# Edge gathers asked for by pairs of tiles, at most 24 tiles ahead, in a two-layer graph network kernel

## Chip, cores and metric

The kernel runs on one core of a Trainium2 chip (trn2). The metric is the device time of one execution in microseconds; three runs of the kernel before gave a median of 3993.59 us.

## The reference

There are 50000 nodes with 128 features and 50000 edges. A first convolution and two message-passing layers all work on the same edge list, which is sorted by destination. Each of the three sums rows over the edges of a destination node:

```python
dst = jnp.minimum((50000 * jax.random.uniform(key3, (50000,)) ** 2.0).astype(jnp.int32), 49999)
_o = jnp.argsort(dst, stable=True)
...
# convolution
h = X * norm_src
agg = jax.ops.segment_sum(h[src], dst, num_segments=N)
...
# each of the two layers
m = jnp.concatenate([h[row], h[col]], axis=-1)
m = jax.nn.relu(m @ msg_W1[l].T + msg_b1[l])
m = m @ msg_W2[l].T + msg_b2[l]
agg = jax.ops.segment_sum(m, col, num_segments=h.shape[0])
upd = jnp.concatenate([h, agg], axis=-1) @ upd_W[l].T + upd_b[l]
h = _layer_norm(h + upd, ln_g[l], ln_b[l])
```

The square in the draw of the destinations makes low node numbers much more frequent: of the blocks of 128 nodes, those at the high end have about 64 edges each and those at node 0 over a thousand.

## The kernel before

The program is a row of stages with a barrier between any two: `rank` and `place` sort the edges, `plan` makes tables, `edges` (the sum of the convolution, with the degrees), `conv`, `nodes`, then `edges0`, `nodes0`, `edges1`, `nodes1`. The three edge stages are one function, `edge_stage` (L764), called with `degrees` true for the first and false for the other two.

The edges stand in TP = 392 **edge tiles** of 128, in the order of their destinations, from the high node numbers to the low ones. The nodes stand in 392 node tiles of 128. A **step** is one edge tile with one node tile that it touches, so there are 784 steps, and four of them make one of the NB = 196 **batches** in which TensorE works. Where nodes have few edges (the start of a stage) a batch uses little more than one new edge tile; where they have many (its end) it uses nearly four.

For each edge tile GpSimd issues one indirect DMA (L851) that gathers the 128 source rows, by index, from a table in memory to a place in `ring`, which has RE = 64 places. So tile e takes the place of tile e - 64 and has to wait until that one is used up. GpSimd works through groups g of four tiles (L842 to L855). From group 16 on it first waits (L847) for the semaphore of the batch in which the last tile of group g - 16 ends; that is `s_seg` in the degrees stage and `s_pq`, which L1013 raises, in the others. The batch numbers come from the table `tile_end`, packed three to a word, of which eight words are loaded every 24 groups (L846). `tile_end` is made in `plan_stage` (L695 to L702) from `full` (L640) and a small matmul (L742), one entry per group. After the four gathers of group g it waits until group g - 2 has landed and tells TensorE so with `s_prow` (`landed`, L838 to L840). After the last group it does this for the last two.

In the degrees stage the first 48 tiles (PRE) were gathered in `plan` (L564) and GpSimd starts with tile 48.

TensorE waits in each batch for `s_prow` at the group of the newest tile it needs (L1007, L1033). In edges0 and edges1 a batch i is `segment(i - 2)` (L1021, eight matmul records) and then `combine(i)` (L1011 and L1012, sixteen records). In the degrees stage it is `sum_rows(i)` (L1036, eight records) with, in turn, a transpose of input rows (L1044) or a product with a weight (L1051) that belong to the convolution. VectorE adds the batch's four results into `acc` (L883) and makes the one-hot tiles (L868), ScalarE makes the turned one-hots and the messages.

Of the kernel before, what the change touches and what calls it, by code (L numbers as in the profile page):

```python
# [5 lines left out]
F32, F16, I32 = mybir.dt.float32, mybir.dt.float16, mybir.dt.int32  # L6
ALU, ACT, AX = mybir.AluOpType, mybir.ActivationFunctionType, mybir.AxisListType

P = 128
# [7 lines left out]
TP = 392  # L17
# [7 lines left out]
NCHUNK = TP // J  # L25
# [13 lines left out]
EW = -(-NCHUNK // 3)  # L39
EPS = 1e-5  # L40
# [475 lines left out]
def plan_stage(nc, m):  # L516

    K = TP // 4
    with ExitStack() as ctx:
# [10 lines left out]
        bound = sb("bound", [K, NCHUNK])  # L530
        cnt_w = sb("cnt_w", [K, 4, P])
        ended, ended1, at_e = sb("ended", [K, 4, S]), sb("ended1", [K, 4, S]), sb("at_e", [K, 4, S], F16)
        full = sb("full", [K, 4, NCHUNK])
# [4 lines left out]
        tf, ends = sb("tf", [1, 3, NCHUNK]), sb("ends", [1, 4, 3 * EW], I32)  # L538
# [10 lines left out]
        with nc.Block() as block:  # L549

            @block.gpsimd
            def _(pool):
# [6 lines left out]
                nc.gpsimd.iota(bound[:], pattern=[[4 * P, NCHUNK]], base=4 * P, channel_multiplier=0,  # L559
# [10 lines left out]
            def _(dve):  # L570
# [51 lines left out]
                nc.vector.memset(m.tile_end[:], 0)  # L622
# [69 lines left out]
                link(nc.vector.tensor_scalar(tf[:, 2, :], sen_row[0:1, 1:1 + TP].rearrange("o (c j) -> o c j", j=4)[:, :, 3], 1.0, None, ALU.add))  # L692
                link(nc.vector.tensor_copy(ends[:, 0, 0:NCHUNK], tf[:, 2, :]))
                dve.wait_ge(s_full, 1)
                link(nc.vector.tensor_scalar(tf[:, 0, :], ps_c[0:1, 2, 0:NCHUNK], float(TP - 1), -1.0, ALU.min, ALU.add))  # L695
                link(nc.vector.scalar_tensor_tensor(out=tf[:, 1, :], in0=bound[0:1, :], scalar=1.0 / P, in1=tf[:, 0, :],
                                                    op0=ALU.mult, op1=ALU.add))
                link(nc.vector.tensor_copy(ends[:, 1, 0:NCHUNK], tf[:, 1, :]))
                link(nc.vector.tensor_scalar(ends[:, 2, 0:NCHUNK], ends[:, 1, 0:NCHUNK], 2, None, ALU.arith_shift_right))
                link(nc.vector.tensor_scalar(ends[:, 3, 0:NCHUNK], ends[:, 2, 0:NCHUNK], 1, None, ALU.add))  # L700
                for k, to in ((0, m.chunk_end), (3, m.tile_end)):
                    pack(to[:, 0:EW], 10, [ends[:, k, :].rearrange("o (w j) -> o w j", j=3)[:, :, j] for j in range(3)], 10)  # L702

            @block.tensor
            def _(pe):
# [35 lines left out]
                for k in range(4):  # L741
                    last = nc.tensor.matmul(ps_c[:, 2, 0:NCHUNK], ones[0:K, :], full[:, k, :], start=k == 0, stop=k == 3)  # L742
# [21 lines left out]
def edge_stage(nc, m, table, table_q, agg, degrees, x=None):  # L764
# [6 lines left out]
    with ExitStack() as ctx:  # L771
# [26 lines left out]
        with nc.Block() as block:  # L798
# [35 lines left out]
            def _(pool):  # L834
# [7 lines left out]
                for g in range(first, NCHUNK):  # L842
                    if g >= RE // 4:
                        k = g - RE // 4
                        if k % 24 == 0:
                            ends = load(mybir.EngineType.Pool, m.tile_end[0:1, k // 3:k // 3 + 8])  # L846
                        pool.wait_ge(s_seg if degrees else s_pq, third(ends, k))  # L847
                        pool.sem_inc(s_go, 1)
# [705 lines left out]
```

## Time and profile before

| | us |
|---|---|
| three runs | 4000.14, 3985.41, 3993.59 (median 3993.59) |
| span of the profiled execution, first to last instruction | 3444.6 |
| median less the span | 549.0 |
| TensorE busy | 2975.2 (86%) |
| VectorE busy | 2700.0 (78%) |
| ScalarE busy | 2379.7 (69%) |
| GpSimd busy | 1846.0 (54%) |
| edges stage, by its gathers | 544.5 to 1003.4 |
| edges0 stage, by its gathers | 1577.4 to 2101.3 |
| edges1 stage, by its gathers | 2532.3 to 3056.9 |

The profile is of one execution and comes with its span; it has no device time of its own, so the three runs stand in the table. What lies outside the span is start and end of the execution. Times in the trace are counted from the span's start. Busy time leaves out waits on semaphores and register work. A GpSimd record of L851 is the making of one gather, not the landing of its data. POOL is GpSimd, PE is TensorE, DVE is VectorE, ACT is ScalarE, SP is SyncE, and a "q" behind a name is the engine's instruction queue.

### The profile page before, as it was taken

To read this page: it belongs to the slowest core of one execution; us is meant where nothing else is said; L and a number is where in the kernel's file an instruction comes from. 1 tells how busy PE (TensorE), PEld (TensorE's weight loads), DVE (VectorE), ACT (ScalarE), POOL (GpSimd) and SP (SyncE) were. 2 spreads that over 40 slices of the span, in tenths; PEclk is the share of its full clock that TensorE was granted. 3 is DMA by queue.
4 is the path that set the end of the run, shared out by engine and by line. 5 is a ranking of instruction groups with operands and counts; after the bars stand their busy time and mean duration, and the time that the engine had idled before them with its cause. 6 is when DMAs were issued, how large, how long until landed. Compare 5 with 4: busy or idle time off the path is not lost. (4 is left out here: it accounts for less than half of the span.)

```text
span 3444.6 us, 92529 instructions
## 1 busy us (share of the span) xinstructions
PE 2975.2 (86%) x25312; PEld 2674.1 (78%) x25312; DVE 2700.0 (78%) x8634; ACT 2379.7 (69%) x5642; POOL 1846.0 (54%) x1782
## 2 busy tenths in 40 slices
PE   4975656777767789997999998999979999989998
PEld 3753334555543378987999998999979999989998
DVE  9999967888856688885777776666657777769998
ACT  3779945777742368886777775666657777759999
POOL 0000036577755533335776776555547767766664
PEclk9999988999979989999999999999989999999999
DMA  0027635777649989997776654999977766548887
GB/s 21 2 69 229 223 103 162 221 219 215 195 139 340 346 280 355 366 356 250 225 221 208 191 158 123 327 327 326 328 239 229 221 210 194 164 129 287 296 295 240
DMA packets 460711, 777.79 MB, mean 226 GB/s; under 512 B 113689, under 2 KB 115865, under 8 KB 460393
## 3 DMA queue, kind: packets, MB, share of 16 engines
q1 hardware_dynamic: 355046, 548.85, 48.2%
q10 hardware_dynamic: 67714, 147.73, 12.5%
q0 software_dynamic: 37632, 77.15, 9.2%
q8 instruction: 178, 2.92, 0.3%
q14 instruction: 141, 1.15, 0.1%
HBM read 451.50 MB, written 321.78 MB: 224 GB/s over the span
## 5 line engine op out<-in xcount | busy, mean ns | idle before, releaser
L883 DVE SCALAR_TENSOR_TENSOR edges_acc<-edges_acc,keep,edges_ps_a 128x128 f32 (+1 forms) x2352 | 820.3, 349 | 272.1 <-issue 145.9
L851 POOL DMA_INDIRECT ring<-table_p,esrc x784 | 787.5, 1004 | 313.3 <-issue 206.0
L1011 PE MATMUL edges_ps_m<-ring,ident 128*128 x3136 | 609.7, 276 | 33.8 <-POOLq L840 33.8
L1012 PE MATMUL edges_ps_m<-edges_q_ring,edges_turned 128*128 x3136 | 608.8, 276 | 0.0
L1011 PEld LDWEIGHTS edges_ps_m<-ring,ident 128*128 128x128 f32 x3136 | 478.6, 193 | 34.7 <-ACT edges_turned L967 17.7
L1012 PEld LDWEIGHTS edges_ps_m<-edges_q_ring,edges_turned 128*128 128x128 f32 x3136 | 478.8, 193 | 0.0
L979 ACT ACTIVATE edges_msg<-edges_ps_m 128x512 f32<-128x512 f32 x392 | 234.2, 597 | 295.5 <-PE edges_ps_m L1012 294.7
L1021 PE MATMUL edges_ps_a<-edges_onehot,edges_msg 128*128 128x128 f32 x3136 | 414.0, 275 | 0.0
L851 POOL DMA_INDIRECT ring<-table_h,esrc x344 | 327.7, 953 | 138.5 <-issue 93.5
L1021 PEld LDWEIGHTS edges_ps_a<-edges_onehot,edges_msg 128*128 128x128 f32 x3136 | 381.7, 192 | 0.0
L868 DVE TENSOR_TENSOR edges_onehot<-iota,drel 128x512 f32<-128x512 f16 x441 | 305.0, 692 | 96.1 <-PE edges_ps_a L1021 94.0
L1286 POOL TENSOR_TENSOR nodes_extra<-ub,deg 128x512 f32<-128x512 f32 x196 | 203.8, 1040 | 285.8 <-DVE nodes_y L1443 244.9
L1036 PEld LDWEIGHTS edges_ps_a<-ring,edges_onehot 128*128 128x128 f32 x1568 | 195.5, 196 | 175.9 <-issue 104.1
L1381 PE MATMUL nodes_ps_y<-uw,nodes_in_a 128*128 128x128 f32 x1568 | 306.0, 277 | 19.4 <-DMA nodes_in_z<-table_z 19.4
L1382 PE MATMUL nodes_ps_y<-wproj,nodes_in_z 128*128 128x128 f32 x1568 | 305.5, 277 | 0.0
L1407 PE MATMUL nodes_ps_p<-wproj,nodes_z_t 128*128 128x128 f32 x1568 | 303.2, 275 | 0.0
L1406 PE MATMUL nodes_ps_q<-wproj,nodes_z_t 128*128 128x128 f32 x1568 | 303.1, 275 | 0.0
L1036 PE MATMUL edges_ps_a<-ring,edges_onehot 128*128 x1568 | 224.0, 287 | 90.8 <-DVE edges_acc L883 47.5
L965 ACT ACTIVATE edges_turned<-edges_d_ring,minus_lane 128x512 f32<-128x512 f16 x392 | 279.3, 712 | 21.8 <-DMA edges_d_ring<-table_d 21.6
L967 ACT ACTIVATE edges_turned<-edges_turned,one 128x512 f32<-128x512 f32 x392 | 283.1, 722 | 12.8
L1454 DVE BATCH_NORM_STATS2 nodes_st<-nodes_y 128x6 f32<-128x128 f32 x1176 | 255.6, 280 | 6.9
L1289 POOL TENSOR_TENSOR nodes_extra<-nodes_extra,bu 128x512 f32<-128x512 f32 x196 | 249.8, 1274 | 15.4
(315 smaller groups left out, 6776.2 us busy)
## 6 DMA issues: line engine op xcount, KB each, us to landing
table_z<-nodes_z_t SPq DMA_DIRECT2D x196, 256.0 KB, 5.0
table_p<-nodes_p_out SPq DMA_DIRECT2D x196, 256.0 KB
table_q<-nodes_q_out ACTq DMA_DIRECT2D x196, 256.0 KB
edges_q_ring<-table_q SPq DMA_DIRECT2D x196, 256.0 KB, 4.8
edges_d_ring<-table_d ACTq DMA_DIRECT2D x98, 512.0 KB
table_t<-edges_acc SPq DMA_DIRECT2D x196, 256.0 KB
nodes_in_a<-table_t SPq DMA_DIRECT2D x196, 256.0 KB
nodes_in_z<-table_z SPq DMA_DIRECT2D x196, 256.0 KB, 4.3
```

The source lines that it names most:

```text
L851: nc.gpsimd.indirect_dma_start(out=ring[:, e % RE * W:e % RE * W + P], out_offset=None, in_=table[:, :], in_offset=bass.IndirectOffsetOnAx ...
L868: nc.vector.tensor_tensor(onehot[:, i % HR, :, :], m.iota[:, 0:P].unsqueeze(1).to_broadcast([P, 4, P]), m.drel[:, 4 * i:4 * i + 4].unsquee ...
L883: nc.vector.scalar_tensor_tensor(out=to, in0=to, scalar=m.keep[:, s:s + 1], in1=ps_a[:, i % AR, where(j):where(j) + F], op0=ALU.mult, op1= ...
L967: nc.scalar.activation(to, to, ACT.Relu, bias=m.one[:], scale=-1.0).then_inc(s_turned, 1)
L1011: nc.tensor.matmul(to, m.ident[:], rows[j], start=True, stop=False)
L1012: last = nc.tensor.matmul(to, turned[:, i % QR, j * P:(j + 1) * P], slots[j], start=False, stop=True)
L1021: last = nc.tensor.matmul(ps_a[:, i % QR, j * P:(j + 1) * P], msg[:, i % QR, j * P:(j + 1) * P], onehot[:, i % HR, j, :], start=True, stop ...
L1036: last = nc.tensor.matmul(ps_a[:, i % AR, where(j):where(j) + F], onehot[:, i % HR, j, :], rows[j], start=True, stop=True)
L1381: nc.tensor.matmul(to, part(in_a, b, j), m.uw[:, layer, :], start=True, stop=False)
L1382: last = nc.tensor.matmul(to, part(in_z, b, j), m.wproj[:, layer, 2 * D:3 * D], start=False, stop=True)
L1406: nc.tensor.matmul(part(ps_q, b % 2, j), part(z_t, b, j), m.wproj[:, nxt, D:2 * D], start=True, stop=True)
L1407: last = nc.tensor.matmul(part(ps_p, b % 2, j), part(z_t, b, j), m.wproj[:, nxt, 0:D], start=True, stop=True)
```

## The change

GpSimd asks for places per pair of edge tiles in place of per group of four, and a tile waits for the batch in which tile e - 24 (and e - 23) ends, not e - 64 (to e - 61). The waits per stage become 184 in edges0 and edges1 (before 82), and 172 in the degrees stage (before 82). The eight words are loaded every 24 pairs, and at the start of the degrees stage as well, where the first wait is for pair 12 (tiles 24 and 25). The ring keeps its 64 places. `landed` stays per group of four. In `plan_stage` the table and its temporaries get 196 entries in place of 98.

```diff
+NPAIR = TP // 2
+PW = -(-NPAIR // 3)
+AHEAD = 24
...
-        bound = sb("bound", [K, NCHUNK])
+        bound = sb("bound", [K, NPAIR])
-        full = sb("full", [K, 4, NCHUNK])
+        full = sb("full", [K, 4, NPAIR])
-        tf, ends = sb("tf", [1, 3, NCHUNK]), sb("ends", [1, 4, 3 * EW], I32)
+        tf, ends = sb("tf", [1, 2, NPAIR]), sb("ends", [1, 4, 3 * PW], I32)
...
-                nc.gpsimd.iota(bound[:], pattern=[[4 * P, NCHUNK]], base=4 * P, channel_multiplier=0,
+                nc.gpsimd.iota(bound[:], pattern=[[2 * P, NPAIR]], base=2 * P, channel_multiplier=0,
...
-                link(nc.vector.tensor_scalar(tf[:, 0, :], ps_c[0:1, 2, 0:NCHUNK], float(TP - 1), -1.0, ALU.min, ALU.add))
+                link(nc.vector.tensor_scalar(tf[:, 0, :], ps_c[0:1, 2, 0:NPAIR], float(TP - 1), -1.0, ALU.min, ALU.add))
...
-                link(nc.vector.tensor_copy(ends[:, 1, 0:NCHUNK], tf[:, 1, :]))
-                link(nc.vector.tensor_scalar(ends[:, 2, 0:NCHUNK], ends[:, 1, 0:NCHUNK], 2, None, ALU.arith_shift_right))
-                link(nc.vector.tensor_scalar(ends[:, 3, 0:NCHUNK], ends[:, 2, 0:NCHUNK], 1, None, ALU.add))
-                for k, to in ((0, m.chunk_end), (3, m.tile_end)):
+                link(nc.vector.tensor_copy(ends[:, 1, 0:NPAIR], tf[:, 1, :]))
+                link(nc.vector.tensor_scalar(ends[:, 2, 0:NPAIR], ends[:, 1, 0:NPAIR], 2, None, ALU.arith_shift_right))
+                link(nc.vector.tensor_scalar(ends[:, 3, 0:NPAIR], ends[:, 2, 0:NPAIR], 1, None, ALU.add))
+                for k, to, w in ((0, m.chunk_end, EW), (3, m.pair_end, PW)):
...
-                    last = nc.tensor.matmul(ps_c[:, 2, 0:NCHUNK], ones[0:K, :], full[:, k, :], start=k == 0, stop=k == 3)
+                    last = nc.tensor.matmul(ps_c[:, 2, 0:NPAIR], ones[0:K, :], full[:, k, :], start=k == 0, stop=k == 3)
...
                 for g in range(first, NCHUNK):
-                    if g >= RE // 4:
-                        k = g - RE // 4
-                        if k % 24 == 0:
-                            ends = load(mybir.EngineType.Pool, m.tile_end[0:1, k // 3:k // 3 + 8])
-                        pool.wait_ge(s_seg if degrees else s_pq, third(ends, k))
-                        pool.sem_inc(s_go, 1)
-                    for j in range(4):
-                        e = 4 * g + j
+                    for e in range(4 * g, 4 * g + 4):
+                        if e % 2 == 0 and e >= AHEAD:
+                            k = (e - AHEAD) // 2
+                            if k % 24 == 0 or e == 4 * first:
+                                ends = load(mybir.EngineType.Pool, m.pair_end[0:1, k // 24 * 8:k // 24 * 8 + 8])
+                            pool.wait_ge(s_seg if degrees else s_pq, third(ends, k))
+                            pool.sem_inc(s_go, 1)
                         nc.gpsimd.indirect_dma_start(
```

## Rows read from the trace of the kernel before

**Rows 1.** The page's head and its first part, whole span.

```profile
span 3444.6 us, 92529 instructions
...
PE 2975.2 (86%) x25312; PEld 2674.1 (78%) x25312; DVE 2700.0 (78%) x8634; ACT 2379.7 (69%) x5642; POOL 1846.0 (54%) x1782
```

**Rows 2.** Stretches of 50 us in edges0; the first line names the columns.

```profile
core 0: us, PE busy (x) PEld busy (x) DVE busy (x) ACT busy (x) POOL busy (x), PEclk, DMA share, GB/s
...
1670.00:1720.00 50.00, 50.00 (x450) 50.00 (x450) 38.68 (x95) 35.75 (x56) 38.42 (x39) 1.00 0.73 225
...
2020.00:2070.00 50.00, 50.00 (x451) 50.00 (x449) 38.40 (x93) 36.46 (x57) 38.59 (x38) 1.00 0.46 141
```

**Rows 3.** Stretches of 20 us at the end of the degrees stage, columns as in rows 2.

```profile
940.00:960.00 20.00, 15.78 (x102) 11.69 (x101) 15.84 (x41) 14.60 (x35) 15.12 (x17) 1.00 0.64 187
...
980.00:1000.00 20.00, 11.12 (x44) 7.46 (x44) 8.66 (x22) 7.24 (x18) 15.12 (x17) 0.67 0.30 82
```

**Rows 4.** L851 alone by stretch: us, POOL busy (gathers), PEclk, DMA share, GB/s.

```profile
1577.40:1921.50 344.10, 255.48 (x256) 0.98 0.71 219
1921.50:2101.40 179.90, 138.60 (x136) 1.00 0.52 156
544.40:782.00 237.60, 159.74 (x168) 0.99 0.78 219
...
2532.30:2877.00 344.70, 254.80 (x256) 0.98 0.71 219
2877.00:3057.00 180.00, 138.60 (x136) 1.00 0.52 156
```

**Rows 5.** L851: duration ns minimum, median and maximum, first and last start.

```profile
L851 POOL DMA_INDIRECT ring<-table_p,esrc x784: 938/944/1444, 1577.4 to 3055.9; - x196
L851 POOL DMA_INDIRECT ring<-table_h,esrc x344: 938/944/1462, 544.5 to 1002.4; - x172
```

**Rows 6.** GpSimd in order of time, edges0: start, length, idle before and its releaser.

```profile
1577.42 0.99 POOL L851 DMA_INDIRECT ring<-table_p,esrc  x1 [21.00 <-POOLq L1527]
...
1581.21 1.44 POOL L851 DMA_INDIRECT ring<-table_p,esrc  x1 [0.30 <-issue]
...
1591.69 0.94 POOL L851 DMA_INDIRECT ring<-table_p,esrc  x1 [0.30 <-issue]
...
1921.57 0.94 POOL L851 DMA_INDIRECT ring<-table_p,esrc  x1 [2.49 <-PE edges_ps_m L1012]
...
2100.38 0.94 POOL L851 DMA_INDIRECT ring<-table_p,esrc  x1 [0.30 <-issue]
```

**Rows 7.** GpSimd in order of time, degrees stage.

```profile
782.06 0.94 POOL L851 DMA_INDIRECT ring<-table_h,esrc  x1 [2.46 <-PE edges_ps_a L1036]
...
1002.43 0.94 POOL L851 DMA_INDIRECT ring<-table_h,esrc  x1 [0.30 <-issue]
```

**Rows 8.** TensorE in order of time, end of the degrees stage.

```profile
985.32 1.13 PE L1036 MATMUL edges_ps_a<-ring,edges_onehot 128*128 x8 [1.27 <-POOLq L840]
990.27 1.16 PE L1036 MATMUL edges_ps_a<-ring,edges_onehot 128*128 x8 [3.38 <-POOLq L840]
...
1006.20 2.06 PE L1036 MATMUL edges_ps_a<-ring,edges_onehot 128*128 x8 [2.21 <-POOLq L840]
...
1008.90 1.93 PE L1036 MATMUL edges_ps_a<-ring,edges_onehot 128*128 x8
```

**Rows 9.** TensorE in order of time, edges0: its first batches and its last two.

```profile
1587.78 0.77 PE L1011 MATMUL edges_ps_m<-ring,ident 128*128 x2 [16.23 <-POOLq L840]
...
2109.08 0.39 PE L1011 MATMUL edges_ps_m<-ring,ident 128*128 x2
...
2111.76 0.39 PE L1011 MATMUL edges_ps_m<-ring,ident 128*128 x2
```

**Rows 10.** VectorE in the plan stage, one row per shape, 533 to 545 us.

```profile
L685 DVE COPY steps<-plan_ti 1x196 int32<-1x196 int32 x2 | 0.9, 449 | 0.1
L696 DVE SCALAR_TENSOR_TENSOR plan_tf<-plan_bound,plan_tf 1x98 f32<-1x98 f32 x1 | 0.2, 249 | 0.0
```

More of the change, by code:

```diff
@@ L621, in _ @@
                 nc.vector.memset(m.chunk_end[:], 0)
-                nc.vector.memset(m.tile_end[:], 0)
+                nc.vector.memset(m.pair_end[:], 0)
                 nc.vector.memset(m.slots[:], 0)
@@ L691, in _ @@
                 nc.vector.tensor_copy(m.slots[:, 0:NB], table[:, :, 1])
-                link(nc.vector.tensor_scalar(tf[:, 2, :], sen_row[0:1, 1:1 + TP].rearrange("o (c j) -> o c j", j=4)[:, :, 3], 1.0, None, ALU.add))
-                link(nc.vector.tensor_copy(ends[:, 0, 0:NCHUNK], tf[:, 2, :]))
+                link(nc.vector.tensor_scalar(tf[:, 0, 0:NCHUNK], sen_row[0:1, 1:1 + TP].rearrange("o (c j) -> o c j", j=4)[:, :, 3], 1.0, None, ALU.add))
+                link(nc.vector.tensor_copy(ends[:, 0, 0:NCHUNK], tf[:, 0, 0:NCHUNK]))
                 dve.wait_ge(s_full, 1)
-                link(nc.vector.tensor_scalar(tf[:, 0, :], ps_c[0:1, 2, 0:NCHUNK], float(TP - 1), -1.0, ALU.min, ALU.add))
+                link(nc.vector.tensor_scalar(tf[:, 0, :], ps_c[0:1, 2, 0:NPAIR], float(TP - 1), -1.0, ALU.min, ALU.add))
                 link(nc.vector.scalar_tensor_tensor(out=tf[:, 1, :], in0=bound[0:1, :], scalar=1.0 / P, in1=tf[:, 0, :],
                                                     op0=ALU.mult, op1=ALU.add))
-                link(nc.vector.tensor_copy(ends[:, 1, 0:NCHUNK], tf[:, 1, :]))
-                link(nc.vector.tensor_scalar(ends[:, 2, 0:NCHUNK], ends[:, 1, 0:NCHUNK], 2, None, ALU.arith_shift_right))
-                link(nc.vector.tensor_scalar(ends[:, 3, 0:NCHUNK], ends[:, 2, 0:NCHUNK], 1, None, ALU.add))
-                for k, to in ((0, m.chunk_end), (3, m.tile_end)):
-                    pack(to[:, 0:EW], 10, [ends[:, k, :].rearrange("o (w j) -> o w j", j=3)[:, :, j] for j in range(3)], 10)
+                link(nc.vector.tensor_copy(ends[:, 1, 0:NPAIR], tf[:, 1, :]))
+                link(nc.vector.tensor_scalar(ends[:, 2, 0:NPAIR], ends[:, 1, 0:NPAIR], 2, None, ALU.arith_shift_right))
+                link(nc.vector.tensor_scalar(ends[:, 3, 0:NPAIR], ends[:, 2, 0:NPAIR], 1, None, ALU.add))
+                for k, to, w in ((0, m.chunk_end, EW), (3, m.pair_end, PW)):
+                    pack(to[:, 0:w], 10, [ends[:, k, 0:3 * w].rearrange("o (w j) -> o w j", j=3)[:, :, j] for j in range(3)], 10)
             @block.tensor
@@ L1505, in build @@
         m.steps, m.slots = sb("steps", [1, 2 * NB], I32), sb("slots", [1, NB + 4], I32)
-        m.chunk_end, m.tile_end = sb("chunk_end", [1, EW + 7], I32), sb("tile_end", [1, EW + 7], I32)
+        m.chunk_end, m.pair_end = sb("chunk_end", [1, EW + 7], I32), sb("pair_end", [1, PW + 7], I32)
         m.esrc, m.elocal = sb("esrc", [P, TP], I32), sb("elocal", [P, TP])
```

## The prediction

> **What bounds the kernel now.** The page comes first: span 3444.6 us, TensorE the busiest engine at 86%, GpSimd the least busy at 54% [rows 1]. That share is an average over stages, so the next view is the stretches. In edges0 TensorE is busy 50.00 of 50 us from shortly after the start to the end, with 450 matmul records, and at 24 records a batch that is 2.67 us a batch; the step from one of the last batches to the next gives 2.68 [rows 2, 9]. So in edges0, and in edges1, which is the same code, TensorE bounds the stage, and nothing that GpSimd does can shorten it. But GpSimd is busy 38.4 of each 50 us in the same rows with 38 or 39 gathers, and almost each gather has 0.30 us of idle before it that waits for nothing [rows 2, 6]. 0.944 and 0.30 make 1.244 us a gather, so 39 gathers fill 48.5 of 50 us: GpSimd has next to no reserve there.
>
> The order of time shows how little. In edges0 the gathers run from 1577.42 to 2100.38, and TensorE's last two batches start at 2109.08 and 2111.76 [rows 6, 9]. The two engines end together. In the degrees stage GpSimd is already behind: from 985 us TensorE stands idle again and again and is released by the note that a group has landed (L840), and it gets its last group at 1006.20, 3.77 us after the last gather began [rows 7, 8].
>
> Where does GpSimd wait for places today? Counting gathers by stretch, 256 were made before 1921.5 us, and the next one, tile 256, waited 2.49 us for TensorE's `combine` [rows 4, 6]. It is the first of group 64 and waits for the batch in which tile 195 ends. From then on no gather waits for a place: 135 spacings take 2100.38 - 1921.57 = 178.8 us, or 1.3245 us each. In the degrees stage 168 gathers stand before 782 us, after 48 made in plan, so tile 216 was the last to wait, for tile 155; the rest take (1002.43 - 782.06)/175 = 1.259 us each [rows 4, 7]. In edges1 the same count, 256 and then 136 in 180.0 us, is found at 2877 us [rows 4].
>
> So the end of each gather sequence is a place released by TensorE plus an unbroken run of gathers. The time at which TensorE is through tile 195 (or 155) is set by TensorE's own pace and stays. What the change alters is how many gathers are left at that moment.
>
> **The change part by part.** Edges0 first. In the new kernel tile 218 waits for the pair (194, 195), so it can't start before 1921.5. After it 173 tiles follow in place of 135, since the lead is 38 tiles shorter (tile 256 before, 218 now). 173 x 1.3245 = 229.1, so the last gather starts at 2150.7 in place of 2100.38: 38 x 1.3245 = 50.3 us later. Edges1 has the same count: 50.3. In the degrees stage the tile that waits for 155 is now 178, 213 are left, and the last gather starts 38 x 1.259 = 47.9 us later. Waits that fall earlier change nothing, because these end the run already.
>
> How much of that reaches the end of the stage? In the degrees stage TensorE already waits for the last group [rows 8], so all 47.9. In edges0 TensorE's batch at 2109.08, the first that needs the last group, started 8.70 us after the last gather began and waited for nothing. From the start of a group's last gather to TensorE's start it takes 3.77 us at the end of the degrees stage [rows 7, 8] and 1587.78 - 1581.21 = 6.57 at the start of edges0 [rows 6, 9]. The reserve is thus 8.70 less 3.77 to 6.57, 2.1 to 4.9 us, and the term 45.4 to 48.2; I take 46, near the value with little other traffic, for edges0 and again for edges1.
>
> Twice as many waits: 102 more a stage in edges0 and edges1, 90 in the degrees stage, each with its register work and an increment, and the loads of eight words. Cover: GpSimd's queue runs ahead of the engine. TensorE was released at 1587.78 by a note that stands in the program behind the twelfth gather, which began at 1591.69 [rows 6, 9]. The added instructions run in that lead, and I take 0. Without the cover the nearest price is one more idle of 0.30 for each added wait: in the run that counts about 43 (edges0, edges1) or 53 are new, 13, 13 and 16 us, together 42 as the upper end. A gain is excluded, since nothing is taken away. What stands behind a waiting request is the note on an older group: with the new lead the note on tiles 4g to 4g+3 goes out only when tile 4g - 13 is used up. That leaves 13 tiles, over three batches at even four tiles a batch, so I cost it at nothing until the run itself is late.
>
> The spacing of the run: each gather takes 938 to 1444 ns [rows 5]. The floor is 0.944 + 0.30 = 1.244, which would take 13.9 us off each of edges0 and edges1 and 3.1 off the degrees stage, 31 in all. The other end is the 1.344 us of the first 344.1 us of edges0, waits included [rows 4]: 3.4 more a stage. I take 1.3245, the same stretch of the same stage.
>
> The rows show why a gather takes 0.94 at one time and over 1.4 at another by no releaser at all. The Trainium skill, page "SBUF — State Buffer", section "SBUF: two separate sides", says that GpSimd can't write DMA descriptors while VectorE runs an instruction that takes both ports. Such delays go by VectorE's instructions, so they would stay the same in sum (10.8 us) and not grow with the run, and the total by that rule would be 6 us lower than mine.
>
> The clock: with TensorE waiting for landings its granted clock can fall. In the degrees stage it was 1.00 with 15.78 of 20 us busy and 0.67 with 11.12 busy, and the same eight records then took 2.06 us in place of 1.13 [rows 3, 8]. In the late edges0 a group of four gathers takes 5.3 us and a batch 2.68, so TensorE would be half busy. What counts is the tail behind the last landing, two batches at 1.2 GHz, 0 to 5.4 us a stage; I take 2 each. The degrees stage has this already.
>
> Plan stage: five instructions on one row go from 98 to 196 entries, 0.249 to at most 0.449 us each [rows 10], 1.0 us; four of `full` and three of packing add a few tenths. Between 0.3 and 1.5; I take 1. The GpSimd work there ends earlier and hides nothing of it.
>
> Sum: 47.9 + 46 + 46 + 4 + 1 = 144.9 us. The profiled span of 3444.6 becomes 3589.5; with the 549.0 that lie around it against the median, 4138.5. I predict **4138 us**, 3.6% slower.
>
> **The rivals.**
> - *The clock falls for the whole late stretch.* With TensorE 45 us late at the end and a batch of 2.68 us against about 4.3 us of gathers, some 28 batches of edges0 wait. At 1.2 GHz each is 5.36 us: 28 x 5.36 = 150 us, against 28 x 2.68 + 45 = 120: 30 more a stage, 60 in two, less the 4 already counted, and up to 8 in the degrees stage: about 4200. For it: the 0.67. Against: at half clock TensorE would be busy all the time, and in edges0 a busy TensorE stands at 1.00 [rows 2].
>  The Trainium skill, page "TensorE: Matmul & The Clock Gate", section "HAM oscillation — how this bites in real kernels", says that short bursts of matmuls with waits for a DMA between them throttle the clock again at each wait, and it would put the time at this rival's.
> - *The gathers get their floor spacing* because traffic is spread: 4138 - 31 = about 4107, within my range.
> - *Not slower.* If the run after tile 218 went at (2100.38 + 4.9 - 1921.5)/173 = 1.063 us a gather or less, the shorter lead would be made good, edges0 and edges1 would end as now, and the degrees stage too at a similar spacing: about 3994. The place is L851 in the last third of each stage, and the point is 1.06. Against it: the shortest possible spacing today is 1.244, in all three stages.
> - *The change does not do what it says.* If the pair table came out too small, the lead would stay near 64 and the time about 3995. The formula is the same with another divisor; I see no reason for it, and it has the smallest chance.
>
> **How the numbers follow.** The forecast's case has 0.78, the clock 0.12, the floor spacing 0.06, not slower 0.03, the idle change 0.01. The low end is the floor spacing with the largest reserve and no clock loss, 4138 - 31 - 5 = about 4101; the high end adds the uncovered waits and the rest of the tail, 4138 + 42 + 7 = 4187. I give 4100 to 4188, which leaves out the clock rival and the last two. A measurement here tells about 0.5% (20 us) from no change. Faster 0.01, the same 0.03, slower 0.96.
>
> **What the new profile would show.** The last gather of the degrees stage near 1051, of edges0 near 2151 + 49 = 2200, of edges1 near 3201; more idle of L851 released by TensorE in each stage, by about 48 us; waits of L1011 and L1036 on L840 in the last 30 to 45 batches, some 45 us a stage; spacing in the last 173 gathers 1.32. If TensorE is not idle near the end of edges0, or if the spacing there is below 1.2, I am wrong. If TensorE is busy at a clock near 0.5 in the last 150 us, the clock rival holds.

## The result, and the profile after

The changed kernel takes 3923.32 us (median of four, 3913.85 to 3925.8). The kernel before, run beside it, took 3990.28 (median of four). The ratio is 0.983 (0.980 to 0.985): 1.7% **faster**, where 4138 us and 3.6% slower were forecast. Two executions of the experiments below lie far outside the others and are left out of the ratios: one of rest64 took 7799 us, and one of before, beside pauseplan, 4423.

The head and first part of the page of after, and the granted TensorE clock in 40 slices:

```profile
span 3924.1 us, 93325 instructions
...
PE 3146.7 (80%) x25312; PEld 2796.9 (71%) x25312; DVE 2686.3 (68%) x8634; ACT 2361.9 (60%) x5642; POOL 1817.9 (46%) x1782
...
PEclk9989968988778999999999997999989999989999
```

The profiled execution of after took 3925.8 us, of which 3924.1 are its span: only 1.7 us lie outside. That can't be set beside [rows 1], where 3444.6 us of span belong to a kernel that runs in 3990. So the first experiment, told here because all else is read against it, was the kernel before once more, unchanged; `before_again` below. Its profiled execution took 3955.6 us with a span of 3953.9:

```profile
span 3953.9 us, 92529 instructions
...
PE 3138.7 (79%) x25312; PEld 2783.0 (70%) x25312; DVE 2683.3 (68%) x8634; ACT 2361.7 (60%) x5642; POOL 1825.0 (46%) x1782
...
PEclk9999969888779999977999989999959999989999
```

The page that the prediction was made from shows an execution that none of the timed ones beside the experiments resembles: each of them has its span on record too, about 2 us under its time. From the first to the last instruction on a stage's own tiles, in us:

| stage | first profile of before | before again | after |
|---|---|---|---|
| rank, place | 231, 237 | 231, 237 | 231, 238 |
| plan | 69 | 100 | 104 |
| degrees edges | 471 | 596 | 610 |
| conv, nodes | 193, 354 | 190, 352 | 196, 350 |
| edges0, nodes0 | 542, 404 | 722, 403 | 696, 404 |
| edges1, nodes1 | 543, 364 | 722, 365 | 696, 364 |

The 509 us by which the two spans of before differ lie in plan and the three edge stages (31, 125, 180 and 179 us; conv and nodes are a few us shorter). Against `before_again` the change gains 26 us in edges0 and 26 in edges1, and loses 14 in the degrees stage and 4 in plan. The two traces are not of one set of runs: before took 3990 us beside after and 3955 as `before_again`, so in sum the stages show some 35 us less of a gain than the times do.

**Edges0 by stretches** answers to [rows 2]. Before again, from its start at 1728 us:

```profile
core 0: us, PE busy (x) PEld busy (x) DVE busy (x) ACT busy (x) POOL busy (x), PEclk, DMA share, GB/s
1728.00:1778.00 50.00, 11.16 (x56) 9.73 (x56) 5.37 (x4) 6.04 (x9) 37.41 (x39) 0.57 0.39 123
1778.00:1828.00 50.00, 16.33 (x81) 14.59 (x82) 8.40 (x21) 8.25 (x14) 27.43 (x29) 0.55 0.25 71
1828.00:1878.00 50.00, 47.74 (x409) 46.41 (x409) 32.29 (x80) 31.72 (x50) 23.37 (x24) 1.00 0.61 195
...
2400.00:2450.00 50.00, 46.69 (x404) 46.50 (x402) 36.86 (x92) 30.13 (x48) 0.00 (x0) 0.97 0.06 22
```

After, from its start at 1749 us, same columns:

```profile
1749.00:1799.00 50.00, 24.87 (x160) 23.42 (x160) 14.32 (x26) 15.87 (x25) 29.13 (x31) 0.67 0.46 153
1799.00:1849.00 50.00, 48.58 (x424) 47.79 (x425) 37.03 (x91) 33.37 (x54) 23.38 (x25) 1.00 0.65 203
...
2395.00:2445.00 50.00, 37.13 (x262) 35.38 (x261) 22.34 (x57) 16.99 (x27) 19.52 (x21) 0.84 0.14 35
```

The gain is at the start. In its first 100 us before makes 137 matmul records, after 584. For those 100 us the kernel before has a GpSimd that makes gather after gather (39 in the first 50 us) and a TensorE that hardly runs. The loss is at the end: in the last 50 us after makes 262 records, with 21 gathers still to come; before makes 404 and has no gather left.

What holds TensorE is seen in its order of time, before again. The columns are start, length, record, and the idle time before it with what ended it; the two ACT lines are ScalarE's message, on which a record of L1021 waits:

```profile
1744.26 0.47 PE L1012 MATMUL edges_ps_m<-edges_q_ring,edges_turned 128*128 x2
...
1750.65 0.27 PE L1012 MATMUL edges_ps_m<-edges_q_ring,edges_turned 128*128 x1 [0.46 <-issue]
1752.76 0.57 PE L1012 MATMUL edges_ps_m<-edges_q_ring,edges_turned 128*128 x1 [1.84 <-issue]
1754.15 0.37 PE L1011 MATMUL edges_ps_m<-ring,ident 128*128 x1 [0.82 <-issue]
1756.25 0.37 PE L1011 MATMUL edges_ps_m<-ring,ident 128*128 x1 [1.73 <-issue]
1758.35 0.37 PE L1012 MATMUL edges_ps_m<-edges_q_ring,edges_turned 128*128 x1 [1.73 <-issue]
1760.45 0.37 PE L1012 MATMUL edges_ps_m<-edges_q_ring,edges_turned 128*128 x1 [1.73 <-issue]
1780.08 0.60 ACT L979 ACTIVATE edges_msg<-edges_ps_m 128x512 f32<-128x512 f32 x1 [33.08 <-DMA table_g<-conv_g_t]
1780.82 2.05 PE L1021 MATMUL edges_ps_a<-edges_onehot,edges_msg 128*128 128x128 f32 x8 [19.99 <-issue]
...
1816.45 0.37 PE L1012 MATMUL edges_ps_m<-edges_q_ring,edges_turned 128*128 x1 [0.33 <-issue]
...
1818.62 0.60 ACT L979 ACTIVATE edges_msg<-edges_ps_m 128x512 f32<-128x512 f32 x1 [36.59 <-PE edges_ps_m L1012]
1819.36 2.05 PE L1021 MATMUL edges_ps_a<-edges_onehot,edges_msg 128*128 128x128 f32 x8 [1.14 <-ACT edges_msg L979]
...
1822.98 0.39 PE L1011 MATMUL edges_ps_m<-ring,ident 128*128 x2
1823.20 0.39 PE L1012 MATMUL edges_ps_m<-edges_q_ring,edges_turned 128*128 x2
```

In the first profile and in all good stretches a record comes every 0.11 us. Here, from 1750 us, one comes about every 2.1 us (0.7 to 4.2), and the profile names no semaphore behind it ("issue"). I call this the crawl. The one hole of 20 us is put down to "issue" as well, but it ends 0.74 us after ScalarE's message starts at 1780.08, just as the wait that the profile does put down to ScalarE ends 0.74 us after 1818.62. So in the hole ScalarE was late, after 33 us of idle: the crawl isn't TensorE's alone. From 1819 us on all is well. GpSimd at that turn, before again:

```profile
1806.82 0.94 POOL L851 DMA_INDIRECT ring<-table_p,esrc  x1 [0.30 <-issue]
1808.07 0.96 POOL L851 DMA_INDIRECT ring<-table_p,esrc  x1 [0.30 <-issue]
1819.65 0.95 POOL L851 DMA_INDIRECT ring<-table_p,esrc  x1 [10.62 <-PE edges_ps_m L1012]
...
2396.80 1.29 POOL L851 DMA_INDIRECT ring<-table_p,esrc  x1 [0.30 <-issue]
```

And after, the same places, which answer to [rows 6]:

```profile
1749.97 0.99 POOL L853 DMA_INDIRECT ring<-table_p,esrc  x1 [20.48 <-POOLq L1529]
...
1779.27 0.94 POOL L853 DMA_INDIRECT ring<-table_p,esrc  x1 [0.30 <-issue]
1784.75 0.95 POOL L853 DMA_INDIRECT ring<-table_p,esrc  x1 [4.54 <-DMA table_g<-conv_g_t]
1786.00 0.95 POOL L853 DMA_INDIRECT ring<-table_p,esrc  x1 [0.30 <-issue]
1790.75 0.95 POOL L853 DMA_INDIRECT ring<-table_p,esrc  x1 [3.80 <-PE edges_ps_m L1014]
...
2424.59 0.95 POOL L853 DMA_INDIRECT ring<-table_p,esrc  x1 [0.30 <-issue]
```

Before, GpSimd makes its 64 gathers at one go and pauses for the first time at 1809, 80 us into the stage. After, it has to stop at 24 and pauses at 1780, 30 us in. TensorE leaves its crawl about 10 us after the last gather of the run in before again (1808 and 1819), and within 6 us in after (1779.3 and 1784.7).

**What comes to TensorE in between.** The page lists, under DMA queues, one for instructions. It is the same line in every run:

```profile
q8 instruction: 178, 2.92, 0.3%
```

178 packets of 16 KB. Their starts, read from the packets in the trace, in edges0:

```
                 length   packets  16 KB packets, us after the stage's start      longest gap
first profile     542       46     21  31  41  55 ...                                21
before again      722       45     56 103 116 128 ...                                56
after             696       45     38  51  62  74 ...                                38
```

The number is fixed by the program, and the rate at which they come is the rate at which TensorE advances: 11.8 us apart in the mean in the first profile, and 4.3 of the 196 batches to a packet. The Trainium skill, page "Advanced Engine Details and Errata", section "ISA Cache", gives an instruction cache of 32 KB (128 KB on TensorE) in lines of 16 KB, which are 256 instructions, and says that there are only two lines. With two records, a load and a matmul, for each of 24 products a batch, 4.3 batches are 204 of 256 instructions. The trace agrees: with its register and semaphore records TensorE has 254 to 256 records to a packet in edges0, in the mean of each of the 14 traces. So the packets are most likely TensorE's instructions.

**Theory F** (fetch), on which the experiments turn: as long as GpSimd makes gathers without a pause, the instruction packets hardly come (one did in before again, 56 us into the run of 64), and TensorE, whose edge stages are straight code, starves. Pauses of GpSimd would let them through. A shorter lead is good because GpSimd pauses sooner at the start of a stage. At the end the opposite holds: waits for places run out, or the gathers are late.

F has two parts. The traces don't bear out the first, that the packets are kept away. Here is how many matmul records TensorE had made in edges0 when the stage's first four packets started:

```
                packet 1     2     3     4
first profile         68   164   253   371
before again          64   167   272   378
after                 67   167   262   370
rest64                66   164   269   368
busy24                67   161   261   376
pause4_64             66   171   256   376
pause8_64             67   141   261   371
```

A packet that had been kept away would start with TensorE further on than elsewhere. It starts at about the same place of TensorE's work in all 14 traces (63 to 69, 141 to 171, 253 to 273, 366 to 378), crawl or no crawl. So the packets follow TensorE, and the long gaps between them are a result of the crawl. In before again the crawl also goes on for over 30 us behind the packet at 56 us (1784), and is over at 1819, 12 us before the next one at 1831. What is left of F is its second part, and the experiments test that: in a run of gathers without a pause TensorE crawls, and pauses keep it from that. What is late in a crawl is not shown.

TensorE's advance in edges0, as microseconds after the stage's start at which it had made a fourteenth, half and 13 of 14 of its matmul records:

```
                    1/14   1/2   13/14   end    first part, middle (12 parts), last part
first profile        51    276    502    542        51   451   40
before again        123    372    681    722       123   558   41
after                70    317    630    696        70   560   66
pairs64             126    373    678    719       126   552   41
groups24             70    321    639    700        70   569   61
pairs16              58    303    620    690        58   562   70
rest64               55    381    690    730        55   635   40
twice24             104    350    666    732       104   562   66
busy24               69    339    655    719        69   586   64
ramp                 64    333    679    720        64   615   41
pause4_64            55    321    581    647        55   526   66
pause4_24            58    305    604    675        58   546   71
pause8_64           122    367    671    712       122   549   41
```

After against before again (two sets of runs, as said): 53 us gained in the first part, nothing in the middle (+2), 25 lost in the last.

### The profile page after: what moved, and what is told of

The parts are those of the page before. It is cut to its first block and busy times, and to the rows that moved or that the text cites. A ratio compares the mean times of both kernels' runs of the same rounds, so it can differ in the third digit from the quotient of the medians.

```text
span 3924.1 us, 93325 instructions
## 1 busy us (share of the span) xinstructions
PE 3146.7 (80%) x25312; PEld 2796.9 (71%) x25312; DVE 2686.3 (68%) x8634; ACT 2361.9 (60%) x5642; POOL 1817.9 (46%) x1782
## 5 line engine op out<-in xcount | busy, mean ns | idle before, releaser
L853 POOL DMA_INDIRECT ring<-table_p,esrc x784 | 760.1, 970 | 640.8 <-PE edges_ps_m L1014 329.8
L1013 PE MATMUL edges_ps_m<-ring,ident 128*128 x3136 | 646.6, 288 | 125.5 <-POOLq L843 50.7
L1014 PE MATMUL edges_ps_m<-edges_q_ring,edges_turned 128*128 x3136 | 632.5, 284 | 27.0 <-issue 26.7
L1013 PEld LDWEIGHTS edges_ps_m<-ring,ident 128*128 128x128 f32 x3136 | 499.1, 200 | 148.4 <-issue 98.0
L1014 PEld LDWEIGHTS edges_ps_m<-edges_q_ring,edges_turned 128*128 128x128 f32 x3136 | 499.4, 200 | 36.0 <-issue 35.6
L1023 PE MATMUL edges_ps_a<-edges_onehot,edges_msg 128*128 128x128 f32 x3136 | 437.4, 284 | 69.6 <-issue 63.1
L1023 PEld LDWEIGHTS edges_ps_a<-edges_onehot,edges_msg 128*128 128x128 f32 x3136 | 397.9, 199 | 82.8 <-issue 81.6
L1038 PEld LDWEIGHTS edges_ps_a<-ring,edges_onehot 128*128 128x128 f32 x1568 | 233.7, 226 | 207.4 <-issue 176.0
L1038 PE MATMUL edges_ps_a<-ring,edges_onehot 128*128 x1568 | 259.1, 318 | 116.8 <-issue 70.2
L931 ACT ACTIVATE edges_onehot<-iota,minus_drel 128x128 f32<-128x128 f16 x588 | 187.3, 390 | 122.4 <-remote 49.7
```

The source lines that it names most:

```text
L853: nc.gpsimd.indirect_dma_start(out=ring[:, e % RE * W:e % RE * W + P], out_offset=None, in_=table[:, :], in_offset=bass.IndirectOffsetOnAx ...
L1013: nc.tensor.matmul(to, m.ident[:], rows[j], start=True, stop=False)
L1014: last = nc.tensor.matmul(to, turned[:, i % QR, j * P:(j + 1) * P], slots[j], start=False, stop=True)
L1023: last = nc.tensor.matmul(ps_a[:, i % QR, j * P:(j + 1) * P], msg[:, i % QR, j * P:(j + 1) * P], onehot[:, i % HR, j, :], start=True, stop ...
L1038: last = nc.tensor.matmul(ps_a[:, i % AR, where(j):where(j) + F], onehot[:, i % HR, j, :], rows[j], start=True, stop=True)
```

## The experiments

All are read against before or after by their diff; "lead" is how many tiles ahead GpSimd may be. The chips differ: before took 3958 us beside the first four and beside the three pause kernels, 3993 beside the next four, 3994 beside the last. Ratios are to before on the same chip.

**before_again**: the file before, unchanged.

> The kernel before, unchanged, for a second profile. Theory A (the first profile of it was of an execution unlike the timed ones): span within 10 us of its device time, near 3988, with edges0 and edges1 each near 700 us in place of 545, and TensorE no longer busy all the time there. Theory B (the trace is right and some 545 us lie outside the span in each execution): span near 3445 again, edges0 545 us.

3955.1 us, ratio 0.9985 (0.996 to 1.001). Its trace stands above. No trace here but the first shows the short form of the stages.

**pairs64**, **groups24**, **pairs16**: the two parts of the change alone, and a shorter lead yet.

pairs64 is after with one line changed, and pairs16 the same with 16:

```diff
-AHEAD = 24
+AHEAD = 64
```

groups24 is before with the lead of 24 (`AHEAD = 24`):

```diff
-                    if g >= RE // 4:
-                        k = g - RE // 4
-                        if k % 24 == 0:
+                    if g >= AHEAD // 4:
+                        k = g - AHEAD // 4
+                        if k % 24 == 0 or g == first:
```

> The changed kernel with AHEAD = 64, so pairs but the old lead. If the shorter lead makes the gain (theory A1): like the kernel before, ratio 0.995 to 1.005, about 3990. If asking by pairs makes it (theory A2): about 3925, ratio 0.983.

> The kernel before with groups of four kept and the lead cut to 24 tiles. If the shorter lead makes the gain (theory A1): about 3925, ratio 0.983. If the pairs make it (theory A2): no gain, or a loss, 3990 to 4130.

> The changed kernel with a lead of 16 tiles. Theory A1 with the shorter lead good in itself: 3900 or less, until TensorE waits for landings; a note on a group needs three groups (12 tiles) asked for, so at 16 only four tiles of reserve are left and I expect waits on L843 to grow to over 50 us a stage and the time to be 3950 to 4100. If what counts were only the number of gathers issued in a burst, it would go on falling to about 3900.

pairs64 3935.3 us, 0.993 (0.990 to 0.995). groups24 3929.6, 0.992 (0.989 to 0.995). pairs16 3903.0, 0.983 (0.980 to 0.987). The two parts multiply to 0.985, about the whole change (0.983). So both theories that I had set against each other miss: neither the lead nor the pairs make the gain alone. Lead 16 gives the same ratio as lead 24 has on its own before, and not the 3950 us or more that I expected for late landings. The lead is what shortens the crawl at the start: 126 us with lead 64, 70 with 24, 58 with 16, by pairs or by groups. It is also what costs the last part 20 to 30 us. Where the gain of the pairs comes from is less clear: at lead 64 edges0 is only 3 us shorter and edges1 5; 10 us are in the degrees stage, and 7 in plan, where the pairs do nothing that could shorten it (it took 93 to 106 us over the kernels with the same gathers in plan).

**rest64**, **twice24**, **busy24**, **ramp**: what is it in GpSimd's run that hurts? rest64 has lead 64, but in the first 16 groups GpSimd waits for each group's own data. twice24 is after with 24 more gathers in a row, into a tile that nothing reads, behind the first 24 of edges0 and edges1; busy24 has 24 additions of 128x512 there instead, which nothing reads either. ramp lets the lead grow from 16 to 64 over the stage. rest64, with `AHEAD = 64` and `REST = 16`:

```diff
-                    if g >= first + RG - 2:
-                        landed(g - (RG - 2))
+                    while told <= g - (0 if g < REST else RG - 2):
+                        landed(told)
+                        told += 1
```

twice24 (in busy24 the loop holds a `tensor_tensor` into `junk` in place of the gather):

```diff
+                    if g == 5 and not degrees:
...
+                        for e in range(24):
+                            nc.gpsimd.indirect_dma_start(
+                                out=junk[:, e * P:(e + 1) * P], out_offset=None, in_=table[:, :],
```

ramp (with `lead(e)` in place of `AHEAD`):

```diff
+def lead(e):
+    return 16 + 2 * (e // 16)
```

> Lead of 64 tiles, but in the first 16 groups GpSimd waits after each group until it has landed, so it pauses a few us every four gathers. Theory F (a run of gathers without a pause keeps the instruction packets away, and TensorE then crawls): the crawl of some 80 us at the start of edges0 and edges1 is gone, the first 14 batches take under 65 us in place of 112, 16 KB instruction packets come every 12 to 20 us from the start, and with the late lead kept the time is 3870 or less, ratio 0.975 or less. Rival R (a long lead itself does the harm, by traffic or by the places): like pairs64, about 3935, ratio 0.993.

> The changed kernel with, in edges0 and edges1, a pause after the first 24 gathers and then 24 more gathers that go to a tile nobody reads, 30 us without a pause, while TensorE has 24 landed tiles to work on. Theory F: TensorE crawls during these 30 us with no 16 KB packet in them; each stage some 15 to 30 us longer than in the changed kernel, 3955 to 3985. Rival R (lead): the lead is 24 as before, no crawl, and each stage under 10 us longer: about 3940.

> As twice24, but the 30 us of GpSimd are 24 vector additions (about 1.04 us each, 25 us) and no gathers. If theory F is about making gathers (descriptors or their packets): the 16 KB packets go on and TensorE keeps its 2.7 to 2.9 us a batch, time near the changed kernel's, 3920 to 3945. If it is GpSimd being occupied at all: the same crawl as in twice24, 3950 to 3985.

> Pairs with a lead that grows from 16 tiles at the start of a stage by 2 each 16 tiles to 64 at its end (22 at tile 48 in the degrees stage). Theory F: the start of the stage is like pairs16 (first 14 batches 47 us) and the last 14 batches go at TensorE's pace, 37 us in place of 63: each of edges0 and edges1 20 to 50 us under the changed kernel, total 3830 to 3880, ratio 0.968 to 0.980. Rival: if late gathers without pauses do the same harm, the growing lead gives it all back: 3900 to 3930.

rest64: 3979.9 us, 0.996 (0.995 to 0.997). Where the rests are there is no crawl: 55 us for the first part, and a packet every 10 to 16 us. But then they stop. GpSimd makes up its lead in one run without a pause from 1848 to 1908, and between 1853 and 1940 no packet comes; in that stretch one fourteenth of the records takes 99 us. The crawl was not removed, it moved to where the run without a pause now is. TensorE makes 114 matmul records between the two packets, about as many as in the other gaps (82 to 136 in this stage), so here too the packet was not late. And the crawl outlasts the run: it ends at 1933, though GpSimd stood still for 4.9 us from 1911 on. One short pause doesn't end it at once. I had expected a gain for the whole stage, so the time was a miss and the place a hit.

twice24: 3991.9 us, 1.001 (0.999 to 1.002), against 0.983 for after: 24 gathers more behind the first 24 cost each stage 36 us, 34 of them in the first part (104 against 70), a little more than the 15 to 30 that I had expected. busy24: 3967.0, 0.992 (0.990 to 0.995). Here GpSimd is kept for about as long by additions, and the first part takes 69 us, as in after; packets start at 1787, 1798, 1809 and 1825, so TensorE goes on at its pace. The time, 3967, lies in the range that I had set for the other reading (3950 to 3985), but the 23 us that edges0 loses come after the additions, when GpSimd makes up the gathers in a run. So it is gathers, not a busy GpSimd, that the crawl goes with.

ramp: 4002.7 us, 1.003 (1.001 to 1.005), a miss. It has after's start (64) and before's end (41), as meant, but the middle takes 615 us in place of 560. A lead that grows is more gathers per batch than TensorE uses up, so GpSimd would pause less all through the stage; that this costs the 55 us is argued and not tested. This ramp, at least, doesn't give the start and the end together.

**pause4_64**, **pause4_24**, **pause8_64**: if any pause will do, then one need not come from a place that is lacking. GpSimd makes one addition of 128x512, which nothing reads, after every fourth (or eighth) gather in the three edge stages, and waits for it before the next one. pause4_64:

```diff
+AHEAD = 64
+EVERY = 4
...
+                def pause(n):
+                    if n:
+                        pool.wait_ge(s_rest, n)
+                    nc.gpsimd.tensor_tensor(rest[:], ..., ALU.add).then_inc(s_rest, 1)
...
+                        if e % EVERY == EVERY - 1:
+                            pause((e - 4 * first) // EVERY)
```

> Lead 64 by pairs, and after every fourth gather GpSimd makes one vector addition of 128x512 (about 1.04 us) that nobody reads; all three edge stages. Theory F: instruction packets get through in these gaps also while gathers run on, the crawl at the start is gone, the spacing is 1.5 us a gather, and edges0 and edges1 take about 600 to 650 us in place of 722: total 3750 to 3870. If about 1 us is too short for a packet to be asked for: crawl as before, total 3990 or more. Rival R (lead): no gain against pairs64, ratio 0.993 or above.

> The same with the lead of 24. Theory F: if the short gaps suffice, less than the changed kernel by the rest of the crawl at the start (some 12 us a stage) and by the late crawls, 3850 to 3900; the late part stays bound by gathers at 1.5 us. If they don't suffice: the changed kernel's time or up to 20 us more, 3920 to 3945.

> As pause4_64 with one addition per eight gathers, spacing 1.38 us. Theory F with gaps of 1 us enough: packets every 11 us at most, 3750 to 3850, below pause4_64 in the late part. If TensorE needs more than one such gap in 11 us: between pairs64 and pause4_64.

pause4_64: **3758.3 us, 0.948 (0.945 to 0.952)**, 5.2% faster than before and well under after. pause4_24: 3870.0, 0.977 (0.973 to 0.981). pause8_64: 3918.6, 0.990 (0.986 to 0.994). The beginning of edges0 in pause4_64, with the columns as above, and GpSimd in it:

```profile
span 3763.7 us, 93477 instructions
...
PE 3079.5 (82%) x25312; PEld 2735.3 (73%) x25312; DVE 2756.0 (73%) x8634; ACT 2362.5 (63%) x5642; POOL 2227.4 (59%) x2064
...
1689.00:1739.00 50.00, 34.53 (x284) 33.86 (x285) 28.93 (x52) 25.99 (x41) 40.66 (x38) 0.82 0.61 202
1739.00:1789.00 50.00, 47.28 (x406) 45.77 (x404) 37.97 (x87) 31.25 (x51) 41.81 (x39) 1.00 0.67 205
```

```profile
1739.43 0.95 POOL L861 DMA_INDIRECT ring<-table_p,esrc  x1 [0.31 <-issue]
1740.40 1.28 POOL L846 TENSOR_TENSOR edges_rest<-ub,bu 128x512 f32<-128x512 f32 x1
1741.84 1.24 POOL L861 DMA_INDIRECT ring<-table_p,esrc  x1 [0.16 <-issue]
1743.38 0.95 POOL L861 DMA_INDIRECT ring<-table_p,esrc  x1 [0.31 <-issue]
1744.63 0.94 POOL L861 DMA_INDIRECT ring<-table_p,esrc  x1 [0.30 <-issue]
1745.88 1.26 POOL L861 DMA_INDIRECT ring<-table_p,esrc  x1 [0.31 <-issue]
```

GpSimd has **more** to do (2227 us busy, not 1825), has the full lead, and TensorE makes 690 records in the first 100 us in place of 137. From the end of one group of four to the next gather there are 1.5 us without a gather, and packets come 23, 36, 46 and 60 us into the stage. Now GpSimd is the one that limits the stage: four gathers take 6.5 us, and 98 groups of four are 637 us of the 647. With the addition after every eighth gather the time for the gathers is less, but the first part still takes 122 us: a pause every 11 us isn't often enough, which F as stated doesn't tell. The additions also slow the gathers: from the first to the 64th of edges0 GpSimd takes 102 us with one after every fourth, 88 after every eighth and 79 with none. Whether the gaps or the slower pace keep the crawl away is not separated; no run makes gathers evenly at 1.6 us. Nor does F say why four with lead 24 is slower than with lead 64. The table gives the place: until halfway it is the faster (305 against 321), but from there to 13/14 it takes 299 us against 260. I read this so: where a batch uses many tiles, a GpSimd that is itself the limit can't afford to wait for places too. No run tests it.

**pauseplan**: the second part of F tried in another stage. In plan, 48 gathers run without a pause beside VectorE's and TensorE's straight code. This is pause4_64 with an addition after every fourth of them too.

```diff
                 for e in range(PRE):
...
+                    if e % EVERY == EVERY - 1:
+                        if e > EVERY:
+                            pool.wait_ge(s_rest, e // EVERY)
+                        nc.gpsimd.tensor_tensor(rest[:], step[:, 0:512], step[:, 0:512], ALU.add).then_inc(s_rest, 1)
```

> The kernel pause4_64 with one addition more: in the plan stage GpSimd makes one addition of 128x512 in fp16 after every fourth of the 48 early gathers (11 pauses among them), which nothing reads. Theory F (while GpSimd issues gathers without a pause the instruction packets of the other engines stay away, and a pause of over 1 us after every fourth gather lets them come): the plan stage, 100 to 104 us in all runs with 48 unbroken gathers against 69 us in the first profile of before, falls to 70 to 85 us although GpSimd does about 20 us more work there; a 16 KB instruction packet comes before the 48th gather (none did in pause4_64 between 473 and 553 us). The three edge stages stay at 553, 647 and 644, so the whole is 3730 to 3745 and the ratio to before about 0.943. Rival (the plan stage is longer for another reason, the pause is a help of the edge stages alone, by room in the DMA queues or other spacing of the data): the plan stage stays at 100 to 105 us or grows, no packet comes before the gathers end, and the time is 3755 to 3765, ratio 0.948 or more.

3761.4 us beside a before of 3994.0: 0.942 (0.939 to 0.944), the best ratio of all, though on another chip than pause4_64 and no shorter in its own time, which I had put at 3730 to 3745. What it was run for came out. Plan takes 78 us in place of 103, though GpSimd's gathers in it take 13 us longer. A packet starts at 521 us where none did before 553; TensorE had made 74 of plan's matmul records then and 75 at 553, so this again tells how fast TensorE got on. The plan stage in stretches, pause4_64 first, then pauseplan:

```profile
473.00:510.00 37.00, 11.85 (x45) 8.95 (x43) 13.36 (x52) 0.00 (x0) 28.59 (x34) 0.55 0.19 49
510.00:550.00 40.00, 9.70 (x21) 5.38 (x22) 10.00 (x38) 0.00 (x0) 19.33 (x21) 0.55 0.13 34
```

```profile
473.00:510.00 37.00, 11.40 (x46) 8.48 (x45) 25.43 (x88) 0.00 (x0) 30.34 (x35) 0.60 0.14 41
510.00:550.00 40.00, 21.10 (x70) 12.17 (x68) 28.96 (x43) 0.96 (x2) 32.55 (x32) 0.76 0.17 47
```

VectorE makes 88 instructions in the first 37 us in place of 52: it too had been slower. The edge stages stay (555, 649, 652).

## Why the prediction was wrong

**The step that failed** is the ground of the whole sum, that the first profile shows what the timed executions do: "with the 549.0 that lie around it against the median". They don't lie around it. In every other profiled execution here the span and the time differ by 1.7 to 2.1 us; what the first profile lacks, 509 us, lies inside, in plan and the edge stages (its execution has no time of its own on record). A gap of 16% between a span and a time was a warning, and I, and the text ahead of the prediction, explained it as start and end without a row for it. All further steps were read from stages of which before again takes 31 us more in plan and 125 to 180 in each of the three edge stages. Two steps turned the forecast of a loss into a miss of the direction, and they follow.

**"TensorE bounds the stage, and nothing that GpSimd does can shorten it"** held in the first profile alone, where it is busy 50.00 of 50 us [rows 2]. In the usual form it is busy 11.2 and 16.3 of the first two 50 us, and how many gathers GpSimd makes without a pause there changes the stage by 36 us (twice24) to 75 us (pause4_64).

**"The time at which TensorE is through tile 195 is set by TensorE's own pace and stays"** falls with it. In after the first part is 53 us shorter, and TensorE keeps that head start through the middle. This is the term that the sum lacks, and no rival had it: "not slower" looked for its gain in the spacing of the gathers.

**The shorter lead costs at the end**: right in kind. After makes its last gather 20 us before the stage's end (2424.6 of 2445) and works at it with TensorE busy 37 of 50 us. But the size was off: 25 us, not 46. Nor do the gathers end 50 us later: counted from the stage's start the last one comes at 675 us in after and at 669 in before again, since TensorE gives the places back 55 us sooner (half its records after 317 us, not 372). And the reserve was taken as 2.1 to 4.9 us, where before again makes its last gather at 2396.8 and ends at 2450, 53 us later, since TensorE is the one that is behind. In the degrees stage, where the whole 47.9 was to arrive, the stage is 14 us longer than before again's.

**"From then on no gather waits for a place"**: not so in the usual form. In edges0 of before again gathers still wait for TensorE late in the stage, here the sixteenth from the end:

```profile
2375.68 0.94 POOL L851 DMA_INDIRECT ring<-table_p,esrc  x1 [1.67 <-PE edges_ps_m L1012]
```

The unbroken run of 135 or 173 gathers on which each term was built isn't there.

**Twice as many waits cost nothing**: in agreement. pairs64, which has them all, is 0.7% faster than before.

**The plan stage, +1 us**: can't be told. It took 100 and 104 us, within the spread of 93 to 106.

**The clock**: I put its rival at 0.12. The granted clock is down at both ends of the stage, 0.57 and 0.55 in the first 100 us of before again, 0.67 in after's first 50, 0.84 in its last 50. In each of these stretches TensorE is idle for part of the time. In the crawl the records are 0.37 us long and the idle before them mostly 1.73, so the lower clock is the small part of the loss there.

**The signs I named**: I wrote that I would be wrong if TensorE weren't idle near the end of edges0, or if the gathers' spacing there were below 1.2 us. It is idle there, and the spacing is above 1.25, and still I was wrong. Both signs belong to the end of the stage, and the gain is at its start.

What stays open is, first, why the first profile was of an execution with no crawl, though GpSimd made its gathers without a pause in it too (the first 64 of edges0 in 83 us, against 79 in before again). A run of gathers without a pause is thus not enough for a crawl; something else differed, and no run shows it. Second, what is late in the crawl. It is not the 16 KB packets. The Trainium skill, page "DMA: Bandwidth & Descriptors", section "Queues, rings and completion order", says that each DMA engine goes round the queues that have work, packet by packet. By that rule a packet of instructions would not stay away for 50 us behind gathers, and the traces agree: the DMA engines are busy 0.39 and 0.25 of the time in the crawl, and no packet starts later in TensorE's work than elsewhere. Third, that the packets are TensorE's instructions is inferred from their number and place, and not read from them. Last, the spans of after and before again differ by 30 us and the two medians of the result by 67; before alone differs by 35 between the two sets of runs, which is nearly all of that, but no trace shows in which stages it lies.

## What to carry to other kernels

Set the span of a profile beside the timed executions before anything is read from it; if they differ by more than a few microseconds, profile again. Where GpSimd makes gathers in a long run beside the work of other engines, look on those engines for idle time that is put down to "issue". If it is there, break the run: an idle addition of 1.3 us after every four gathers took 5% off this kernel, the whole change of this document 1.7% and its shorter lead alone 0.8%. The pauses must be there all along, not only at the start. And before a gap in one record is called a cause, count how far the engine had got at each end of it: a gap in its supply and a slow engine look the same against time.

## What the runs showed of the hardware

- While GpSimd makes gathers every 1.25 us without a pause, TensorE falls from a record every 0.11 us to one every 0.7 us or a multiple of it (1.4, 2.1, 2.8), with a hole of 20 us in before again, at whose end it is ScalarE that was late. DMA engines are far from full in that time (0.25 to 0.39 of their time). The first profile is the exception: there the same run of gathers did not do this.
- The 16 KB instruction packets come one to 254 to 256 TensorE records in the mean, and start at the same place of TensorE's work whether it crawls or not. Gaps of 56 us (before again) and 87 us (rest64) between them are a sign of a slow TensorE, and not its cause.
- 24 additions of GpSimd in a row don't bring the crawl about; packets came 11, 11 and 16 us apart beside them.
- 1.5 us without a gather after every four gathers is enough, the same after every eight isn't (first part 55 against 122 us); gap and slower pace are not told apart.
- One kernel can have two profiles that differ by 509 us of 3954 with the same instructions, and of 14 profiles here only the first is of the short form.
